# Attention output divided inside the attention stage, and the capacity search on transposed gates

## What is computed

```python
# 16 heads of 32; 8 experts, 2 per token, capacity 640
attn = softmax(where(causal, q @ k.T / sqrt(32), -inf))
y = (attn @ v).reshape(b, s, d) @ w_o          # residual added outside
probs = softmax(xf @ w_router)
g, eidx = top_k(probs, 2)                      # ties: lower index first
masked = where(fe[None, :] == arange(E)[:, None], fg[None, :], -inf)
vals, idx = top_k(masked, CAP)                 # each expert keeps its best 640
xe = xf[tok_of[idx]]
ye = relu(xe @ w1) @ w2 * gates                # scattered and added back
```

## Time and profile before

| what | us |
|---|---|
| median of 3 runs | 2489.9 (2489.74 to 2499.09) |
| the profiled execution | 2498.51 |
| its span | 2496.5 |
| PE busy / DVE busy in the span | 2117.8 / 1490.0 |

### The profile page before, as it was taken

The page is one execution under the profiler, slowest core; times in us unless marked ns, Lnnn a source line. Parts: engine busy times, 40 slices in busy tenths (PEclk is TensorE's granted clock), DMA queues, the critical chain, the costliest instruction groups (busy, mean ns, idle before and its releaser), DMA issues. The chain is left out here.

```text
span 2496.5 us, 42717 instructions
## 1 busy us (share of the span) xinstructions
PE 2117.8 (85%) x18144; PEld 1242.3 (50%) x18144; DVE 1490.0 (60%) x2300; ACT 1091.3 (44%) x1070; POOL 531.6 (21%) x445
## 2 busy tenths in 40 slices
PE   6799999999978999799999999965830699999990
PEld 3444444444433444344444444422620688888880
DVE  7768888888856667476666666503352343434323
ACT  5678888888852323134444444440200332222210
POOL 0000000000002114334555555553205000000005
PEclk9899999999988999589999999987755799999995
DMA  6312112112113117530300400025103433333307
GB/s 253 135 43 71 44 64 71 48 60 71 51 58 149 44 66 304 117 85 18 85 19 18 102 18 22 6 51 136 51 0 134 177 114 110 114 110 114 110 26 273
DMA packets 91917, 221.30 MB, mean 89 GB/s; under 512 B 10320, under 2 KB 19664, under 8 KB 84912
## 3 DMA queue, kind: packets, MB, share of 16 engines
q1 hardware_dynamic: 80640, 176.50, 22.0%
q0 software_dynamic: 11088, 42.08, 4.7%
HBM read 154.72 MB, written 59.51 MB: 86 GB/s over the span
## 5 line engine op out<-in xcount | busy, mean ns | idle before, releaser
L449 ACT ACTIVATE m_step<-m_ub,gat_bias 128x2048 bf16<-128x2048 f32 x256 | 493.9, 1992 | 119.4 <-DVE m_mask L526 109.0
L1144 DVE TENSOR_REDUCE t_rm<-t_m 128x1 f32<-128x512 f32 (+3 forms) x640 | 375.8, 609 | 208.7 <-PE t_m L1193 129.2
L1104 ACT ACTIVATE t_E<-t_s 128x1024 f32<-128x1024 f32 (+3 forms) x320 | 277.6, 894 | 376.8 <-PE t_s L1213 187.3
L526 DVE TENSOR_TENSOR m_mask<-m_step,gat_adjT 128x2048 bf16<-128x2048 bf16 x256 | 306.7, 1222 | 82.3 <-ACT m_step L449 72.1
L1083 POOL TENSOR_TENSOR t_total<-t_E 128x1024 f32<-128x1024 f32 (+2 forms) x160 | 307.7, 1935 | 174.5 <-PE t_d L1237 174.5
L1193 PE MATMUL t_m<-t_K,t_Q 96*128 96x512 f32 (+3 forms) x640 | 276.5, 454 | 36.8 <-DVE t_rm L1144 16.8
L1193 PEld LDWEIGHTS t_m<-t_K,t_Q 96*128 96x128 f32 x640 | 126.4, 202 | 192.2 <-DVE t_rm L1144 125.0
L566 PE MATMUL m_bd<-m_mask,m_S 128*32 128x512 bf16 x3072 | 211.3, 379 | 8.0 <-DVE m_mask L526 7.8
L566 PE MATMUL m_bd<-gat_adjT,m_S 128*32 128x512 bf16 x3072 | 211.3, 379 | 4.8 <-PE m_dn L566 4.8
L566 PE MATMUL m_bd<-m_mask,m_neg 128*32 128x512 bf16 x3072 | 211.2, 379 | 0.0
L1210 PE MATMUL t_s<-t_Q,t_K 97*128 97x512 f32 (+3 forms) x640 | 209.8, 404 | 0.5 <-ACT t_E L1104 0.5
(11 more groups left out here) (270 smaller groups left out, 3280.1 us busy)
## 6 DMA issues: line engine op xcount, KB each, us to landing
a_adj<-in_adj SPq DMA_DIRECT2D x16, 1024.0 KB, 5.1
m_ub<-scratch_uac SPq DMA_DIRECT2D x16, 1024.0 KB, 4.8
e_w1r<-in_L_ffn_w SPq DMA_DIRECT2D x8, 2048.0 KB, 8.3
e_w2r<-in_L_ffn_w SPq DMA_DIRECT2D x8, 2048.0 KB, 8.8
t_Q<-scratch_parts SPq DMA_DIRECT2D x48, 256.0 KB, 4.7
scratch_xe<-o_zeros POOLq DMA_DIRECT2D x10, 1024.0 KB, 4.9
e_xe<-scratch_xe SPq DMA_DIRECT2D x8, 1280.0 KB, 9.0
scratch_ye<-e_ye POOLq DMA_DIRECT2D x40, 256.0 KB, 2.3
```

Of the source, the lines that this page charges most:

```text
L449: act.activation(step[n % RELUS][:, :], ub[h % 2][:, :], ACT.Relu, bias=bias[:, j, h:h + 1], scale=BIG).then_inc(step_ready, 1)
L526: dve.tensor_tensor(mask[n % MASKS][:, :], step[n % RELUS][:, :], adjT[:, j, :], ALU.min).then_inc(mask_ready, 1)
L1104: act.activation(E[n % 3][:, two, off:BANK], ps_s[:, two, off:BANK], ACT.Exp, scale=SCALE).then_inc(exp_done[z], 1)
L1144: dve.tensor_reduce(rm[:, h, t, ch:ch + 1], ps_m[i % 2][:, 0:w], AX, ALU.max).then_inc(entry_read, 1)
```

## The change

Attention: DVE divides each unit itself, in five turns (`divide(u, r)`), one behind the entries of each of five following steps. Turn r multiplies part r-1 of `out` (128 columns) by the inverted denominators and inverts part r. The turns of a unit are put on the list four steps behind its last one, the last unit's behind everything. SP stores a unit as one transfer once it is divided, later than before in its list. The router loads the divided output in four transfers of 128 partitions, the first ahead of W and three behind; `share`, `by` and the product are gone, and PE waits for W and the block.

Slots: the two best experts come from two rounds of maximum and comparison on 128x128 operations. The gates are transposed once, so that each of 128 partitions holds one tile and expert. A round tests three candidates, so it settles two bits, and there are 15 (`BITS` 28, 26 .. 0). Each candidate is one `tensor_scalar` of 128x128 that compares and adds up along the row (`accum_out`). PE adds the 16 rows of an expert with the matrix `same` (3 columns). At the end the threshold is transposed back into PSUM (`ps_l`), from which `over`, `tie` and `hit` are made. The ranks' comparison `is_equal` per choice gives way to `chosen[c]`.

```diff
-                    cut = slice(c * BANK, (c + 1) * BANK)
-                    sp.wait_ge(o_copied, u + 1)
-                    for h in range(G):
-                        row = (q * G + h) * OUT
-                        sp.dma_start(o_dram[row:row + DH, cut], out[u % 2][h * DH:(h + 1) * DH, :]).then_inc(o_sent[u % 2], 16)
-                    sp.wait_ge(d_copied, u + 1)
-                    for h in range(G):
-                        row = (q * G + h) * OUT + DH
-                        sp.dma_start(o_dram[row:row + 1, cut], den[u % 2][h * DH:h * DH + 1, :]).then_inc(d_sent[u % 2], 16)
+                    sp.wait_ge(normed, 4 * (u + 1))
+                    sp.dma_start(o_dram[q * P:(q + 1) * P, c * BANK:(c + 1) * BANK], out[u % 2][:, :]).then_inc(o_sent[u % 2], 16)
...
+                    if q:
+                        store(q - 1, 3)
+                    maxima(q, 2)
                     store(q, 0)
-                    maxima(q, 2)
                     if more:
                         load_q(q + 1, 1)
                     store(q, 1)
                     maxima(q, 3)
                     if more:
                         load_q(q + 1, 2)
+                        maxima(q + 1, 0)
                     store(q, 2)
                     if more:
-                        maxima(q + 1, 0)
                         maxima(q + 1, 1)
                         load_q(q + 1, 3)
                     if q + 2 < QUADS:
                         load_k(q + 2)
-                    store(q, 3)
...
-                    act.wait_ge(d_sent[u % 2], 64 * (u // 2))
+                    act.wait_ge(normed, 4 * (u - 1))
...
+                PARTS, WIDE = 4, BANK // 4
+                def divide(u, r):
+                    if r > 0:
+                        part = slice((r - 1) * WIDE, r * WIDE)
+                        dve.wait_ge(inverted, u * PARTS + r)
+                        if r == 1:
+                            dve.wait_ge(o_copied, u + 1)
+                        dve.tensor_tensor(out[u % 2][:, part], out[u % 2][:, part], den[u % 2][:, part],
+                                          ALU.mult).then_inc(normed, 1)
+                    if r < PARTS:
+                        part = slice(r * WIDE, (r + 1) * WIDE)
+                        if r == 0:
+                            dve.wait_ge(d_copied, u + 1)
+                        dve.reciprocal(den[u % 2][:, part], den[u % 2][:, part]).then_inc(inverted, 1)
...
+                        n = q * NS + s - 4
+                        if n >= 0 and n % NS in END.values():
+                            turn += [(n // NS * NC + STEPS[n % NS][0], r) for r in range(PARTS + 1)]
...
+                        if turn:
+                            divide(*turn.pop(0))
                     own, coming = coming, 0
                 copy(QUADS - 1, NC - 1)
+                for r in range(PARTS + 1):
+                    divide(QUADS * NC - 1, r)
...
-                ov = o_dram.rearrange("(h d) n -> h d n", d=DH + 1)
-                sp.dma_start(share[:, :], ov[:, DH, :].rearrange("h (b q) -> h b q", b=P // H)).then_inc(den_in, 16)
-                ok = ov.rearrange("(k g) d n -> g d k n", k=KD)
-                for c in range(NC):
-                    for g in range(P // DH):
-                        sp.dma_start(oT[g * DH:(g + 1) * DH, :, c * BANK:(c + 1) * BANK],
-                                     ok[g, 0:DH, :, c * BANK:(c + 1) * BANK]).then_inc(o_in[c], 16)
+                ov = o_dram.rearrange("(k p) n -> p k n", p=P)
+                def load_o(c):
+                    cut = slice(c * BANK, (c + 1) * BANK)
+                    sp.dma_start(oT[:, :, cut], ov[:, :, cut]).then_inc(o_in[c], 16)
+                load_o(0)
                 sp.dma_start(W[:, :, :], w_o.rearrange("(k p) n -> p k n", p=P)).then_inc(w_in, 16)
-                sp.dma_start(grow[:, :], g2.partition_broadcast(P)).then_inc(w_in, 16)
-                sp.dma_start(Wr[:, :, :], w_router.rearrange("(k p) n -> p k n", p=P)).then_inc(w_in, 16)
+                for c in range(1, NC):
+                    load_o(c)
+                sp.dma_start(grow[:, :], g2.partition_broadcast(P)).then_inc(g_in, 16)
+                sp.dma_start(Wr[:, :, :], w_router.rearrange("(k p) n -> p k n", p=P)).then_inc(wr_in, 16)
...
-                pool.wait_ge(share_ready, 1)
-                pool.dma_start(rec_dram.rearrange("h (b q) -> (h b) q", b=P // H), share[:, :]).then_inc(share_out, 16)
-                pool.wait_ge(share_out, 16)
-                rv = rec_dram.rearrange("(k g) n -> g k n", k=KD)
-                for c in range(NC):
-                    if c >= 2:
-                        pool.wait_ge(o_ready, c - 1)
-                    for g in range(P // DH):
-                        pool.dma_start(by[c % 2][g * DH:(g + 1) * DH, :, :],
-                                       rv[g, :, c * BANK:(c + 1) * BANK].partition_broadcast(DH)).then_inc(by_in[c % 2], 16)
...
-                pe.wait_ge(w_in, 48)
+                pe.wait_ge(w_in, 16)
                 for t in range(T):
                     if t % 4 == 0:
-                        pe.wait_ge(o_ready, t // 4 + 1)
+                        pe.wait_ge(o_in[t // 4], 16)
...
-                dve.wait_ge(den_in, 16)
-                dve.reciprocal(share[:, :], share[:, :]).then_inc(share_ready, 1)
                 for t in range(T):
-                    if t % 4 == 0:
-                        c = t // 4
-                        dve.wait_ge(o_in[c], 16 * (P // DH))
-                        dve.wait_ge(by_in[c % 2], 16 * (P // DH) * (c // 2 + 1))
-                        part = oT[:, :, c * BANK:(c + 1) * BANK]
-                        dve.tensor_tensor(part, part, by[c % 2][:, :, :], ALU.mult).then_inc(o_ready, 1)
...
+                lk(dve.tensor_reduce(fold[:, :], ident[:, :].rearrange("p (t e) -> p e t", e=E), AX, ALU.add))
+                lk(dve.tensor_copy(same[:, :, :], fold[:, None, :].to_broadcast([P, T, E])))
+                dve.sem_inc(same_ready, 1)
+                wide = lambda a: a[:, :, :].to_broadcast([P, T, E])
+                for c, value in enumerate((prob, left)):
+                    lk(dve.tensor_reduce(top[:, :, :], value[:, :, :], AX, ALU.max))
+                    lk(dve.tensor_tensor(best[:, :, :], value[:, :, :], wide(top), ALU.is_equal))
+                    lk(dve.tensor_tensor(weight[:, :, :], best[:, :, :], place_of[:, :, :], ALU.mult))
+                    lk(dve.tensor_reduce(top[:, :, :], weight[:, :, :], AX, ALU.max))
+                    lk(dve.tensor_tensor(chosen[c][:, :, :], weight[:, :, :], wide(top), ALU.is_equal))
+                    if c == 0:
+                        lk(dve.scalar_tensor_tensor(left[:, :, :], chosen[0][:, :, :], -2.0, prob[:, :, :], ALU.mult, ALU.add))
+                lk(dve.tensor_tensor(sel[:, :, :], chosen[0][:, :, :], chosen[1][:, :, :], ALU.add))
                 lk(dve.tensor_tensor(G[:, :, :], prob[:, :, :], sel[:, :, :], ALU.mult))
+                dve.sem_inc(G_ready, 1)
                 lk(dve.memset(thr[:, :], 0))
+                dve.tensor_scalar(cand[:, :], number[:, :], BITS[0], None, ALU.logical_shift_left)
+                dve.wait_ge(G_turned, 1)
+                lk(dve.tensor_copy(GT[:, :], ps_g[:, 0:P]))
...
                 for n, bit in enumerate(BITS):
-                    lk(dve.tensor_scalar(cand[:, :], thr[:, :], 1 << bit, None, ALU.bitwise_or))
-                    dve.tensor_tensor(hit[:, :, :], G[:, :, :],
-                                      cand[:, None, :].bitcast(F32).to_broadcast([P, T, E]), ALU.is_ge).then_inc(hit_ready, 1)
-                    dve.wait_ge(counted, n + 1)
-                    lk(dve.tensor_reduce(room[:, :], ps_c[:, 0:T * E].rearrange("p (t e) -> p e t", e=E), AX, ALU.add))
-                    lk(dve.tensor_scalar(more[:, :], room[:, :], CAP - 0.5, None, ALU.is_gt))
-                    lk(dve.copy_predicated(thr[:, :], more[:, :], cand[:, :]))
-                line = thr[:, None, :].bitcast(F32).to_broadcast([P, T, E])
-                dve.tensor_tensor(over[:, :, :], G[:, :, :], line, ALU.is_gt)
-                dve.tensor_tensor(tie[:, :, :], G[:, :, :], line, ALU.is_equal)
-                lk(dve.tensor_tensor(hit[:, :, :], G[:, :, :], line, ALU.is_gt))
+                    for k in range(K):
+                        dve.tensor_scalar(passed[:, k, :], GT[:, :], cand[:, k:k + 1].bitcast(F32), None, ALU.is_ge, ALU.add,
+                                          accum_out=count[:, k:k + 1]).then_inc(passed_ready, 1)
+                    if n + 1 < len(BITS):
+                        lk(dve.scalar_tensor_tensor(base[:, :], number[:, :], BITS[n + 1], thr[:, :].to_broadcast([P, K]),
+                                                    ALU.logical_shift_left, ALU.bitwise_or))
+                    dve.wait_ge(added, n + 1)
+                    lk(dve.tensor_scalar(more[:, :], ps_c[:, 0:K], CAP - 0.5, None, ALU.is_gt))
```

(15 more changed lines are left out.)

87 lines of the change are left out of this document (44 added, 43 removed).

## The result

The changed kernel took **2459.1 us** (median of four runs, 2457.9 to 2466.8) beside 2493.3 us for the kernel before on the same chip: ratio 0.987, 95% interval 0.984 to 0.990. The forecast was 2457 in a range of 2441 to 2476.

A forecast was written before the change was run, and what follows sets the result against it. PE was taken to set the pace in the attention, a chain of PE and DVE in the slots stage. 18 - 21.4 - 11.5 - 18.2 = -33.1 us, from the median 2489.9 to 2457, range 2441 to 2476.

The forecast's parts named there:

- The attention, +18: Attention: division turns on DVE that overrun their gaps make PE late, 18 us over 70 turns; bounds near 0 and 69.
- its sign: Attention: if the forecast is right, PE waits for DVE by 15 to 20 us more and the stage grows as much.
- the price of the product: Attention: a product of 128 columns on DVE takes 0.29 us, like the two-input hit operation in the slots stage.
- from overrun to PE's lateness: Attention: a turn longer than DVE's gap makes DVE late by the excess, and PE as late; 5.4 us in the second pass.
- The end of the attention, -21.4: Last denominators' copy to first output matmul: division and store add 4.5 us, but PE starts at 1686.5 against 1707.9.
- The router's stalls, -11.5: Router's output matmuls: the stalls between blocks, 4.87, 3.33 and 3.32 us, vanish without the 128x2048 product; tiles every 3.43 us.
- The slots, -18.2: Slots stage: -0.5 us ahead of the search, -18.4 in it (15 rounds of 2.0 us), +0.75 behind it.
- The open point: Slots search: whether DVE's sum along the row is a second instruction; as one instruction each, 4 us lower.
- The turns weren't hidden: Rival, attention: overruns fall into PE's own slack of about 20 us, so it pays 3, not 18: 2442; chance 0.12.
- Each overrun costs the clock too: Rival, attention: twelve overruns each bring a half-clock stretch losing 1.7 us, 20 us more: 2477; chance 0.17.
- W came early: Opposed rival, router start: W arrives late beside other transfers, PE starts at 1702.7, +16: 2473; chance 0.06.
- DVE did not become the bound: Opposed rival, attention: DVE becomes the bound and its 69 us show whole, +18 in all: 2508, slower; chance 0.04.

The follow-up runs named there:

- Experiment 5: Changed kernel with the output weights W loaded behind all four blocks of the attention's result, not behind the first: 2469.6 us (two runs).
- experiment 7: Changed kernel with the search's passes without their sums (no accumulator output, output not the reference's): 2458.6 us, slots stage 45.2 us.

## Why the prediction was right or wrong

**The attention, +18: the size held, its parts didn't.** In the two traces the stage grew by 12.9 us. The same attention ran in six profiles here (670.3, 675.6, 675.1, 671.0, 669.6 and 675.4 us, mean 672.8), and by the mean it grew by 15.4; of the kernel before there is only one. The difference between the profiles goes with the half-clock stretches: four in the three short ones, six or seven in the long ones. What brings them isn't known. Of the twelve second and third passes of this code, seven with one stretch took 156.9 to 157.0 us, three with two 158.0 to 159.7, two with three 161.3: 1.0 to 2.7 us for a second one, 4.3 for two more. PE's wait for t_rm grew by 13.6 us (30.4 against 16.8), a little under the 15 to 20 that the prediction gave as its sign.

Free of that, the turns cost 5.2 us a pass (157.0 against 151.8 with one stretch), where the prediction said 5.4. This agreement is in part luck. With one-input stand-ins for the products the turns cost 2.9 us a pass (154.7 against 151.8), and the remaining 2.3 go with the products that end behind POOL's sums (3.7 us of lengthening a pass, of which 2.3 reach PE). The step that failed is the price of the product: I took the 0.29 of such an operation from the slots stage, where POOL does nothing, while in the attention POOL is busy half of the time. The step that was too dear is the one from overrun to PE's lateness. A turn is also 0.10 us shorter than its parts, since the reciprocal starts 0.20 us behind the product's start. With 0.87 + 0.20 for it the same arithmetic gives, as an estimate, 4.2 us a pass, and on the odd steps 7.3, or 8.6 by another reading of the gaps; measured were 2.9 and 4.2 (156.0 against 151.8). PE thus absorbs some third to half of the overruns so counted. Which of its waits does so wasn't settled.

The Trainium skill has the rule that I should have weighed (SBUF — State Buffer, § Who interferes with whom): a DVE instruction with two inputs in SBUF contends with a GpSimd instruction that reads SBUF, because its second input comes through a read interface that the two share, and the lock on it is exclusive. The trace agrees: 25 long products, each done 0.15 to 0.16 us behind the end of a sum of POOL's, and none long with one input. Nearly all of the wait falls on DVE: the longest sum of POOL's took 2.49 us with the turns and 2.39 without. With that rule weighed the forecast for this stage would have been higher and further from the measured growth: with each product's length as the new trace shows it, the gap arithmetic gives about 24 us, an estimate.

**The end of the attention, -21.4: right.** The last division took 4.8 us, forecast 4.9 (1683.63 to 1688.47), and the first router transfer left 4.9 us later than before, relative to ACT's copy (forecast 4.5). PE started 8.0 us behind it, forecast 9.0, as W landed in 7.6 us (forecast 8.8). Experiment 5 shows that this hangs on W's place in the order.

**The router's stalls, -11.5: right** (-12.1). Tiles come every 3.43 us across blocks. The 0.6 us beyond the forecast are the first tile, whose result came 6.2 us behind the first matmul in place of 6.9. This term had no experiment of its own; all kernels here keep the new router and show 56.7 to 58.2 us.

**The slots, -18.2: right in the sum and in the parts.** Ahead of the search 6.35 us (forecast 6.4), the search 30.1 (30.0), 2.02 a round (2.0). Behind it the hop to PE took 0.63 us (0.7). The open point, whether the sum along the row is a second instruction, was decided by the new trace, which has 45 rows of such a read. By experiment 7 the sums cost 3.1 us in all, where the prediction had 4 for the reads; part of the 3.1 may be the longer passes.

**The rivals.** The turns weren't hidden (5.2 us a pass), though part of each was. "Each overrun costs the clock too" didn't hold for the changed kernel: four to seven stretches against seven before. It holds as a tendency where stalls are many and long (twenty stretches with doubled reciprocals, ten on the odd steps). W came early, and DVE did not become the bound.

## What to carry to other kernels

Work moved beside a bound engine is paid by its place: read the gap behind each position, and put the pieces where the gap holds them. Here that was worth 4.0 of the 5.2 us that the turns cost a pass, some of it because the even steps also met fewer of POOL's sums (9 long products in place of 25); the two shares weren't separated on the even steps. The product of two SBUF tiles on DVE was priced here by what POOL did at that moment (0.28 to 2.5 us), not by its length in a quiet stage. The last piece of moved work stands alone on the path, so let it run under the next stage's loads.

## What the runs showed that I had not expected

- Products of 128 columns took 0.28 to 2.5 us, by whether a sum of POOL's on SBUF was running; the end of a long one was 0.15 to 0.16 us behind that sum's each time. None of 128 maxima over one SBUF input was held up.
- A pass that also sums costs 0.07 us more than one that doesn't, though its read is drawn under the next pass: 0.27 us apart with sums, 0.20 without. The pass's own row is 0.06 longer with them.
- Unchanged code (six profiles of one attention) differs by 6 us, and goes with half-clock stretches of 3.4 us that come in other places and numbers. A difference of that size between two profiles of a stage proves nothing before they are counted.
